# A layer-norm affine step moved behind the blend, and the score matmuls moved behind one common wait

## The reference

```
xn = layernorm(x)
q, k, v = xn @ Wq, xn @ Wk, xn @ Wv          # 8 heads of 64, segments of 256 tokens
for each segment (in order):
    sq = elu(q) + 1;  sk = elu(k) + 1
    att_mem = sq @ mem / (sq @ z)            # memory of the segments before
    mem, z  = mem + sk^T @ v,  z + sum(sk)
    att = softmax(q @ k^T / 8) @ v
    att = gate * att_mem + (1 - gate) * att
y = x + att @ Wo + sqrt((xn @ cos(th + thn))^2 + (xn @ sin(ph + phn))^2)
```

## Time and profile before

| | value |
|---|---|
| median of 9 runs (lowest to highest) | 1470.69 us (1465.64 to 1471.79) |
| the profiled execution's own time | 1470.93 us |
| its span (slowest core, core 3) | 1469.3 us; the other cores 1458.6 to 1469.3 us |
| mean granted TensorE clock of the cores | 0.767 to 0.774 of full speed |
| busy share of the span | TensorE matmul 52%, VectorE 51%, ScalarE 23%, GpSimd 15% |
| the chain that ended last | TensorE 37%, VectorE 29%, ScalarE 12%, DMA 8%, issue 7%, VectorE's own drains (DVEq) 5% |

### The profile page before, as it was taken

The page is one execution under the profiler, slowest core; times in us unless marked ns, Lnnn a source line. Parts: engine busy times, 40 slices in busy tenths (PEclk is TensorE's granted clock), DMA queues, the critical chain, the costliest instruction groups (busy, mean ns, idle before and its releaser), DMA issues.

```text
span 1469.3 us, 14748 instructions; the slowest of 8 cores (1458.6 to 1469.3 us)
## 1 busy us (share of the span) xinstructions
PE 760.4 (52%) x5125; PEld 410.4 (28%) x5125; DVE 751.8 (51%) x1409; ACT 336.2 (23%) x829; POOL 226.2 (15%) x127
## 2 busy tenths in 40 slices
PE   0300157574646556474746556465646465564754
PEld 0200033242424233241423232232324232332421
DVE  2000546565664656565655646565656646566541
ACT  1111303122130403122130403131221304031222
POOL 1111001102030211111030301111120302011113
PEclk9755558687887968796877869796978878696977
DMA  9567000010101010010101010100101010100001
GB/s 172 143 154 157 4 29 2 3 58 1 60 1 58 2 58 3 14 46 1 60 0 58 2 58 2 58 2 1 60 0 60 1 58 2 58 2 7 25 1 57
DMA packets 18123, 56.51 MB, mean 38 GB/s; under 512 B 1217, under 2 KB 5249, under 8 KB 18050
## 3 DMA queue, kind: packets, MB, share of 16 engines
q0 software_dynamic: 8000, 20.97, 7.1%
q1 hardware_dynamic: 10050, 34.59, 6.6%
HBM read 41.98 MB, written 16.78 MB: 40 GB/s over the span
## 4 chain that ended last, share of the span: by engine, by line
PE 37%; DVE 29%; ACT 12%; DMA 8%; issue 7%; DVEq 5%; POOL 1%; ACTq 1%; POOLq 0%
PE pb L123 10%; PE pb L491 8%; ACT e_bf L319 8%; PE pb L370 6%; DVE pT_sb L641 5%; DVE negm L612 4%; PE pb L381 4%; PE pb L393 3%; DVE m2t L657 3%; DVEq L656 3%; DVE attT_bf L679 2%; DVE xnT_sb L564 2%; DMA stage<-th 2%; PE pb L433 2%; DVE out_sb L158 2%
## 5 line engine op out<-in xcount | busy, mean ns | idle before, releaser
L253 POOL TENSOR_TENSOR stage<-fscr 128x1024 f32<-128x1024 bf16 x32 | 62.9, 1964 | 1070.4 <-ACT fscr L138 835.5
L123 PE MATMUL pb<-sin_r,xnT_sb 128*128 128x512 bf16 x512 | 143.6, 444 | 97.2 <-ACT fscr L138 97.2
L319 ACT ACTIVATE e_bf<-pb,negms 128x256 bf16<-128x256 f32 x256 | 117.2, 483 | 170.9 <-DVE negms L617 170.9
L491 PE MATMUL pb<-wo_r,attT_bf 128*128 128x512 bf16 x256 | 113.2, 622 | 71.4 <-DVE attT_bf L679 71.4
L123 PE MATMUL pb<-cos_r,xnT_sb 128*128 128x512 bf16 x512 | 147.7, 454 | 0.0
L421 PE MATMUL pb<-kT_bf,qT_bf 64*128 64x256 bf16 x256 | 33.3, 280 | 203.3 <-DVE v_bf L584 105.5
L641 DVE CAST pT_sb<-pb 128x512 bf16<-128x512 f32 x128 | 79.5, 684 | 114.4 <-PE pb L433 114.4
L370 PE MATMUL pb<-xnT_sb,wq_b 128*128 128x256 bf16 x512 | 87.2, 352 | 81.0 <-DVE xnT_sb L564 59.1
L307 ACT ACTIVATE scr<-scr 128x1024 f32<-128x1024 f32 x16 | 16.9, 1057 | 465.5 <-DVE scr L572 465.5
L138 ACT ACTIVATE fscr<-pb 128x512 bf16<-128x512 f32 x128 | 73.1, 596 | 147.0 <-PE pb L123 134.2
L123 PEld LDWEIGHTS pb<-sin_r,xnT_sb 128*128 128x128 bf16 x512 | 54.7, 111 | 185.8 <-issue 149.0
(11 more groups left out here) (92 smaller groups left out, 1166.3 us busy)
## 6 DMA issues: line engine op xcount, KB each, us to landing
x_sb<-x SPq DMA_DIRECT2D x16, 1024.0 KB, 5.1
y<-out_sb SPq DMA_DIRECT2D x16, 1024.0 KB, 5.3
stage<-th POOLq DMA_DIRECT2D x2, 1024.0 KB, 21.6
stageB<-th POOLq DMA_DIRECT2D x2, 1024.0 KB, 23.0
stage<-thn POOLq DMA_DIRECT2D x2, 1024.0 KB, 10.9
stageB<-thn POOLq DMA_DIRECT2D x2, 1024.0 KB, 12.1
stage<-ph POOLq DMA_DIRECT2D x2, 1024.0 KB, 7.3
stageB<-ph POOLq DMA_DIRECT2D x2, 1024.0 KB, 7.0
```

Of the source, the lines that this page charges most:

```text
L123: li = t_.matmul(pb[6 + half][:, :], xnT_sb[:, ppf + 256 * dt + 128 * u: ppf + 256 * dt + 128 * u + 128], w_s[:, 1024 * dt + 512 * half: 1 ...
L253: g.tensor_mul(stage[:, 0:1024], fscr[:, 0:1024], fscr[:, 0:1024])
L319: sc.activation(e1_bf[:, 2048 * u + 256 * h: 2048 * u + 256 * h + 256], sl, AF.Exp, bias=negms[:, c:c + 1], scale=0.125, accum_out=den[:, ...
L491: li = t_.matmul((bh0 if half == 0 else bh1)[:, :], attT_bf[:, 128 * ft:128 * ft + 128], wo_r[:, 1024 * ft + 512 * half: 1024 * ft + 512 * ...
```

## The change

Two edits, both only of order and waits. On TensorE, the three waits that let the scores of u = 0 start piece by piece (heads 0 and 2 after the first half of v is copied, heads 4 and 6 after the second half, heads 1, 3, 5, 7 after sk) become two waits ahead of all eight: for both halves of v and for sk. The same two waits stand before u = 1 as well, where they have long been met. On VectorE, `bn_xn_affine(t + 1)` is called not after the u = 1 copy of the transposed probabilities but after the blend of u = 0, ahead of the wait for the Wo product of u = 0. No arithmetic changes.

```
                 for u in range(2):
+                    t_.wait_ge(s_ve, 2 * t + 2)
+                    t_.wait_ge(s_sk, t + 1)
                     if u == 1:
                         t_.wait_ge(s_pte, 2 * t + 1)
                     for h in (0, 2, 4, 6, 1, 3, 5, 7):
-                        if u == 0:
-                            if h == 0:
-                                t_.wait_ge(s_ve, 2 * t + 1)
-                            elif h == 4:
-                                t_.wait_ge(s_ve, 2 * t + 2)
-                            elif h == 1:
-                                t_.wait_ge(s_sk, t + 1)
...
                     li.then_inc(s_pte, 1)
-                    if u == 1 and t + 1 < nch:
-                        bn_xn_affine(t + 1)
...
                     li.then_inc(s_bl, 1)
+                    if u == 0 and t + 1 < nch:
+                        bn_xn_affine(t + 1)
                     v.wait_ge(s_wo, 2 * t + u + 1)
```

## The result

The changed kernel is faster: 1410.43 us, median of its runs (1406.86 to 1421.56), against 1470.49 us for the kernel before on the same chips; the ratio is 0.9603, with a 95% interval of 0.9588 to 0.9617. On the 1470.69 us shown at the start that is 0.9603 x 1470.69 = 1412.3 us, 21 us above the forecast of 1391 us and 0.3 us outside the range's upper end of 1412, which is less than the interval can tell.

What follows compares the result with a forecast made beforehand. The prediction took a chain passing between engines as the bound, with VectorE waiting for GpSimd in each chunk. 69.6 - 6.3 + 16.8 = 80.1 us off 1470.93 us gave 1391 us, range 1374 to 1412.

Steps and rivals of the forecast that it cites:

- The affine leaves its old place: VectorE behind the u = 1 copy: waits on GpSimd go, 5.30 us in twelve chunks, 3.0 in two, 69.6 us gained.
- The affine at its new place: VectorE between blend and first addition: covered by 3.61 us before Wo's result is needed, so no cost.
- the cover is used up: Wo wholly at the upper clock level: cover about half, the affine sets that step's end, only the clock's gain lost there.
- The scores behind one wait: TensorE's eight scores of u = 0 start after a 4.24 us gap: 0.42 us a chunk, 6.3 us lost.
- The clock elsewhere: q product and sine block of u = 1: shorter chunks meet the lower clock less, 1.2 us each, 16.8 us gained.
- a sign against it: Sine block of u = 0 on TensorE slowing to over 5 us would show the prediction wrong.
- the rival in which the clock stays with the same blocks: TensorE's q product and sine block keep meeting the lower clock: 63.3 us gained, 1408 us; chance 0.24.
- The wait on GpSimd that stays: Line 657 starts behind GpSimd's second operation: 2.3 us a chunk back, 35.7 us gained, 1435 us; chance 0.05.
- wider loss of the clock: Lower clock spreads over the chunk's first half on TensorE: some 1.9 us a chunk longer, 1498 us; chance 0.03.

Runs made afterwards that it cites:

- the cut of its columns: The changed kernel with the affine of chunks 1 to 15 cut to 8 of 1024 columns: 1408.87 us, ratio 0.9595 to the kernel before.
- the fastest version: Kernel before with only the affine moved, spare matmuls in nearly all TensorE gaps, 16 ahead of each sine block: 1290.01 us, ratio 0.8766.
- the repeat: The changed kernel measured once more, nothing altered: 1411.27 us, ratio 0.9585 to the kernel before.
- the one fill: The changed kernel with eight spare matmuls in TensorE's gap ahead of the sine block of u = 1: 1411.7 us, ratio 0.9589 to before.
- the run with nearly every gap filled: Kernel before with only the affine moved, spare matmuls in nearly every gap, 9 ahead of the u = 0 sine block: 1306.91 us, ratio 0.8868.

## What the prediction had right, and the step that failed

- **The affine leaves its old place** (forecast 69.6 us; measured 14 x 4.77 = 66.8 us): right. Line 657 of u = 0 takes 0.83 us in the mean (0.77 in chunk 7) and the wait of 3.49 us is gone. The small rest is about what the reference explains that I took: in the last chunk of before, the Wo product ran in 3.30 us, after in 3.50 us in the mean over the 84 chunks (3.57 in chunk 7), 14 x 0.20 = 2.8 us. Timelines of TensorE, before and after:

```profile
1415.76 3.30 PE L491 MATMUL pb<-wo_r,attT_bf 128*128 128x512 bf16 x8 [2.23 <-DVE attT_bf L679]
```

```profile
734.58 3.57 PE L486 MATMUL pb<-wo_r,attT_bf 128*128 128x512 bf16 x8 [2.22 <-DVE attT_bf L672]
```

- **The affine at its new place** (forecast nothing): right, by the cut of its columns and by the 2.02 us that are left of the cover. At the upper level the cover is used up, as the prediction had it: in the fastest version the affine takes 2.16 us, ends 0.04 us behind Wo in this chunk, and the addition follows without a wait.

```profile
684.40 2.16 DVE L570 TENSOR_SCALAR xn_bf<-x_sb,rstd,negmr 128x1024 bf16<-128x1024 f32 x2
686.70 0.69 DVE L710 TENSOR_TENSOR out_sb<-x_sb,pb 128x512 f32<-128x512 f32 x1
```

- **The scores behind one wait** (forecast 6.3 us lost): the sign and the 4.24 us gap were right, the size was not. I took the upper bound for every chunk; the eight scores took 0.62, 1.05 and 0.85 us in chunks 4, 5 and 7, and the mean of the stretch grew by 0.06 us by this edit and by 0.20 us in all (14 x 0.20 = 2.8 us). The first two, with the cosine and sine blocks of u = 0 behind them (TensorE's timeline, core 7):

```profile
462.94 0.62 PE L416 MATMUL pb<-kT_bf,qT_bf 64*128 64x256 bf16 x8 [4.24 <-DVE sk_bf L589]
463.50 5.31 PE L123 MATMUL pb<-cos_r,xnT_sb 128*128 128x512 bf16 x16
471.26 3.61 PE L123 MATMUL pb<-sin_r,xnT_sb 128*128 128x512 bf16 x16 [2.45 <-ACT fscr L138]
```

```profile
539.09 1.05 PE L416 MATMUL pb<-kT_bf,qT_bf 64*128 64x256 bf16 x8 [4.59 <-DVE sk_bf L589]
540.07 4.73 PE L123 MATMUL pb<-cos_r,xnT_sb 128*128 128x512 bf16 x16
548.15 5.30 PE L123 MATMUL pb<-sin_r,xnT_sb 128*128 128x512 bf16 x16 [3.35 <-ACT fscr L138]
```

  In the first case the scores were still at the upper level and the fall met the cosine block, which has room before the sine block. In the second the scores were caught, and the sine block of u = 0 as well: what the prediction's last part named as a sign against it (over 5 us) came in 17 of 84 chunks, against 7 before.

- **The clock elsewhere** (forecast 16.8 us gained): this is the step that failed. That a chunk shorter by 5 us meets the lower level less, 1.2 us a chunk, did not come: measured, the stretches other than the scores' and the affine's give 4.9 - 2.8 = 2.1 us lost, about nothing. The sine block of u = 1 got through in 5 of 84 chunks (1 before), but the q product took over 5.9 us in 29 (7 before), and the sum of the three blocks is 14.63 us against 14.33. I read 0.92 us in chunk 9 as a gain of a shorter chunk; it was one case of falls that land elsewhere in single chunks, and the half of the chunk that I read it from, from addition to addition, gained 11.23 - 10.99 = 0.24 us in the mean. The row that should have decided was the gap itself, which the change does not close: 4.06 us ahead of the q product in chunk 7.

```profile
678.74 5.32 PE L370 MATMUL pb<-xnT_sb,wq_b 128*128 128x256 bf16 x32 [4.06 <-DVE xnT_sb L559]
```

  In the mean of the 84 chunks the gap ahead of the sine block of u = 1 is 3.78 us (3.80 before) and that ahead of the q product 3.5 us (3.9 before). A shorter gap alone did not help: it was under 3 us ahead of the q product in 28 chunks, and in 23 of these the product still took 4.9 us or more. That is the rival in which the clock stays with the same blocks, 1408 us, with the amendment that the falls change places among these blocks and nearly keep their sum. With its scores' term at the 2.8 us measured it would have said 1470.9 - 69.6 + 2.8 = 1404 us. That the first term was 2.8 us too large and the loss by the scores 3.5 us too large, so that the two errors cancel, is luck; the miss of the sum is the clock's term, 16.8 + 2.1 = 18.9 us.

- **The other rivals.** The wait on GpSimd that stays did not come in the changed kernel; it comes with fills, and was 0.37 us away. No wider loss of the clock came: TensorE's mean clock is 0.771 to 0.778, in the repeat 0.764 to 0.775 (0.767 to 0.774 before).

What stays open is what decides which block a fall meets. With the one fill, the sine block of u = 1 fell in all 84 chunks with a gap of 2.30 us ahead of it and in none of the 28 with 0.61 us or less; but why the cosine block ahead of it was caught in just those 28 is not shown. In the run with nearly every gap filled, the sine block of u = 0 fell in 51 of 84 chunks behind gaps of 2.0 to 2.4 us and not in the other 33. The runs show only that these falls ended when nearly all gaps were closed.

## What to carry to other kernels

When an operation's mean is far above what it takes in a quiet chunk, look at what GpSimd does at that moment, and put the operation where TensorE's next product covers it; here that was worth 4.8 us of each chunk's 82. Do not count on a better clock from a shorter chunk while the idle gaps ahead of the slow blocks stay: here the falls changed their place, and the sum of the slow blocks hardly. Closing nearly all of the gaps with spare matmuls was worth twice the change under study, closing one gave nothing and closing two 22 us. Spare matmuls that run late can cost: 0.98 us a chunk where they stood ahead of Wo at the lower level.

## What the runs showed of the hardware that was not expected

- Spare work made the kernel faster: 1755 matmuls that nobody needs, 409.7 us of TensorE, brought the mean granted clock from 0.77 to 0.935 and the time from 0.96 to 0.877 of the kernel before.
- A shift of 0.54 us between two engines decides 1.5 us: m2t starting 0.35 us ahead of GpSimd's second operation took 0.76 us, starting 0.19 us behind it 2.26 us.
- Closing one gap from 4.13 to 2.30 us left the block behind it at 5.30 us; where the gap came down to 0.61 us the block took 3.61 us, and the fall moved onto the next products (1.07 us at 0.50 in place of 0.64).
